# DLRM tower on one core: the Gram products spread, quad by quad, between the records of picks and of layer 1

## The reference

```
e = stack([tbl_f[ids[:, f]] for f in 0..31], axis=1)      # 2048 x 32 x 256, fp32
z[b, (i,j)] = dot(e[b, i], e[b, j]) for all i < j          # 496 dots a sample
h = concat([z, dense_ctx], axis=1)                         # 496 + 16 columns
h = relu(h @ W_top1 + b_top1)                              # 512 -> 512
h = relu(h @ W_top2 + b_top2)                              # 512 -> 256
y = h @ W_top3                                             # 256 -> 1
```

## Time and profile before

| what | value |
|---|---|
| median of three runs | 666.28 us (663.17 to 668.51) |
| the profiled execution's own time | 661.49 us |
| its span, first to last instruction | 659.5 us |
| mean granted TensorE clock | 0.966 |
| TensorE: matmuls busy, weight loads busy | 562.8 us (85%), 513.6 us (78%) |
| GpSimd, VectorE, ScalarE busy | 415.1 us, 297.7 us, 247.4 us |
| HBM read | 70.65 MB |

### The profile page before, as it was taken

One profiled execution on the slowest core, in us unless ns is written; L12 is line 12 of the kernel. 1 busy time (PEld: TensorE's weight loads), 2 busy tenths in 40 slices (PEclk: granted clock), 3 DMA queues, 4 the chain that ended last, 5 costly groups with the idle time before them and its releaser, 6 DMA issues.

```text
span 659.5 us, 26697 instructions
## 1 busy us (share of the span) xinstructions
PE 562.8 (85%) x12304; PEld 513.6 (78%) x12304; DVE 297.7 (45%) x556; ACT 247.4 (38%) x496; POOL 415.1 (63%) x435
## 2 busy tenths in 40 slices
PE   1453888999899999999898998999899899986885
PEld 0342888988888888999797988889798888885775
DVE  2144365556435355655435555654435555423041
ACT  1252244444243343433343343433334343334361
POOL 6787577766657576675757566675657667575400
PEclk9995799999999999999999999999999999998987
DMA  5559554433424243342534244242523333232200
GB/s 153 203 193 243 178 151 124 113 99 89 130 83 115 82 116 112 88 124 83 134 87 118 85 105 121 83 122 85 131 79 113 99 90 115 79 108 75 66 12 4
DMA packets 26244, 72.39 MB, mean 110 GB/s; under 512 B 8023, under 2 KB 8935, under 8 KB 25256
## 3 DMA queue, kind: packets, MB, share of 16 engines
q0 software_dynamic: 20544, 56.13, 30.7%
q1 hardware_dynamic: 5590, 14.57, 6.9%
HBM read 70.65 MB, written 0.01 MB: 107 GB/s over the span
## 4 chain that ended last, share of the span: by engine, by line
PE 76%; issue 10%; POOL 6%; ACT 5%; DMA 2%; DVE 1%; SPq 0%; ACTq 0%
PE ps_l L331 17%; PE ps_gram L298 16%; PE ps_pick L276 13%; PE ps_pick L278 12%; PE ps_turn L263 12%; POOL rows L249 6%; PE ps_l L344 4%; DMA rows<-in_table,index 2%; ACT cols L501 1%; ACT pairs L521 1%; DVE pairs L647 1%; ACT cols L467 1%; ACT stage L494 1%; ACT hidden L511 0%; PE ps_turn L361 0%
## 5 line engine op out<-in xcount | busy, mean ns | idle before, releaser
L249 POOL DMA_INDIRECT rows<-in_table,index x428 | 414.3, 968 | 210.5 <-issue 107.0
L647 DVE COPY pairs<-ps_gram 32x112 f32<-32x112 f32 (+1 forms) x480 | 180.6, 376 | 146.1 <-PE ps_gram L298 140.0
L471 ACT COPY cols<-ps_turn 128x512 f32<-128x512 f32 x194 | 114.6, 592 | 254.3 <-PE ps_turn L263 252.9
L263 PE MATMUL ps_turn<-identity,rows 128*128 128x128 f32 x856 | 142.4, 290 | 43.4 <-DMA rows<-in_table,index 41.3
L276 PE MATMUL ps_pick<-one_hot,table_hi 125*128 125x256 f32 x672 | 174.4, 297 | 1.0 <-ACT stage L494 0.8
L635 DVE TENSOR_TENSOR one_hot<-ps_wide,row_number 125x2048 fp32r<-125x2048 f32 x42 | 96.2, 2291 | 162.3 <-ACT ps_wide L488 139.0
L278 PE MATMUL ps_pick<-one_hot,table_lo 125*128 125x256 f32 x672 | 166.9, 286 | 0.0
L263 PEld LDWEIGHTS ps_turn<-identity,rows 128*128 128x128 f32 x856 | 102.5, 147 | 55.9 <-DMA rows<-in_table,index 34.8
L298 PE MATMUL ps_gram<-cols 128*32 128x32 f32 x7936 | 116.1, 202 | 32.4 <-issue 24.4
L298 PEld LDWEIGHTS ps_gram<-cols 128*32 128x32 f32 x7936 | 94.5, 111 | 58.9 <-issue 51.3
L276 PEld LDWEIGHTS ps_pick<-one_hot,table_hi 125*128 125x128 f32 x672 | 129.9, 193 | 2.2 <-issue 1.5
(11 more groups left out here) (51 smaller groups left out, 115.1 us busy)
## 6 DMA issues: line engine op xcount, KB each, us to landing
rows<-in_table,index POOLq DMA_INDIRECT x428
pick_id<-in_pick_ids SPq DMA_DIRECT2D x21, 250.0 KB
stage<-in_tbl SPq DMA_DIRECT2D x4, 1000.0 KB
w_sb<-in_w_t SPq DMA_DIRECT2D x1, 2048.0 KB, 28.5
w_sb<-in_tbl SPq DMA_DIRECT2D x2, 1000.0 KB
w_sb<-in_W_top SPq DMA_DIRECT2D x1, 512.0 KB
pairs<-in_dense_t SPq DMA_DIRECT2D x16, 8.0 KB, 1.6
scores<-score SPq DMA_DIRECT2D x16, 0.5 KB
```

Of the source, the lines that this page charges most:

```text
L249: pool.indirect_dma_start(out=rows[x % ROWS][:, k, :], out_offset=None, in_=table, in_offset=bass.IndirectOffsetOnAxis(ap=index[:, t, i:i ...
L263: last = pe.transpose(ps_turn[x % TURNS][:, h, SPG * k:SPG * (k + 1), :], rows[x % ROWS][:, k, h * P:(h + 1) * P], identity[:, :])
L471: act.copy(cols[t % COLS][:, :, :, FPU * u:FPU * (u + 1)], ps_turn[x % TURNS][:, :, :, :]).then_inc(cols_ready, 1)
L647: last = dve.tensor_copy(pairs[n % 2][N_FIELDS * q:N_FIELDS * (q + 1), c0:KC, TQ * j + FQ * u:TQ * j + FQ * (u + 1)] .rearrange("p c g -> ...
```

## The change

Nothing is added to or taken from what is computed. Four things move:

1. `pick` and `layer1` get three more arguments and call `gram` for a single quad after every second step c of their own loop, that is after every 4 of their 16 matmuls. Eight calls of a pair of blocks carry 4 quads each: in an even block the picks in units 0, 1, 3 and 4, in an odd block the second half of the pick (unit 1) and layer 1's parts in units 2, 3 and 4. `gram_parts` keeps bursts for block 1 (four quads in each of units 1 to 4), four quads in block 29 and the last two blocks.
2. TensorE's picks go to units 0, 1, 3 and 4 of even blocks and to units 0 and 1 of odd ones; layer 1's four parts go to units 2 to 5, layer 2 from unit 3 to unit 2, layer 3 from unit 6 to unit 5.
3. ScalarE's `take_pick`, `spread_ids`, `place`, `relu1`, `relu2` and `take_score` follow to the matching units. `relu1` is now in unit 5, ahead of `evacuate` of unit 6; `place` is in unit 5 for every block from 4 on.
4. VectorE makes both one-hot columns of an even block ahead of that block's `regroup`.

```diff
     def gram_parts(t):
         if t >= BLOCKS - 2:
             return {0: (0, FQ // 2), 1: (FQ // 2, FQ)}
-        return {2: (0, 8), 3: (8, 16)} if t % 2 == 1 else {0: (0, 6), 1: (6, 11), 3: (11, 16)}
+        if t < 2:
+            return {u: (4 * u - 4, 4 * u) for u in range(1, 5)}
+        if t == BLOCKS - 3:
+            return {1: (0, 4)}
+        return {}
...
-            def pick(q, h):
+            def pick(q, h, b=0, g0=0, quads=0):
...
-                if h == HALVES - 1:
-                    last.then_inc(picked, 1)
+                    if c == VC - 1 and h == HALVES - 1:
+                        last.then_inc(picked, 1)
+                    if c % 2 == 1 and c // 2 < quads:
+                        gram(b, g0 + c // 2, g0 + c // 2 + 1)
...
-            def layer1(n, m0=0, m1=M1C):
+            def layer1(n, m0=0, m1=M1C, b=0, g0=0, quads=0):
...
-                if m1 == M1C:
-                    last.then_inc(l1_done, 1)
+                        if c == KC - 1 and m == M1C - 1:
+                            last.then_inc(l1_done, 1)
+                        if c % 2 == 1 and c // 2 < quads:
+                            gram(b, g0 + c // 2, g0 + c // 2 + 1)
...
-                    if 3 <= t < BLOCKS - 1 and t % 2 == 1:
-                        if u == 0:
-                            layer1((t - 3) // 2, 0, 1)
-                        if u == 1:
-                            layer1((t - 3) // 2, 1, 2)
-                        if u == (4 if t == BLOCKS - 3 else 6):
-                            layer1((t - 3) // 2, 2, M1C)
+                    if t % 2 == 1 and jobs(t):
+                        if u in (0, 1):
+                            pick(jobs(t)[0], u, t - 1, 0, 4 * u)
+                        if u in (6, 7) and len(jobs(t)) == 2:
+                            pick(jobs(t)[1], u - 6)
+                    if 3 <= t < BLOCKS - 1 and t % 2 == 1 and 2 <= u < 2 + M1C:
+                        layer1((t - 3) // 2, u - 2, u - 1, t - 1, 4 * (u - 1), 4 if u < 5 else 0)
+                    if t % 2 == 0 and jobs(t):
+                        if u in (0, 1):
+                            pick(jobs(t)[0], u, t - 1, 4 * u, 4)
+                        if u in (3, 4):
+                            pick(jobs(t)[1], u - 3, t - 1, 4 * (u - 1), 4)
                     if 4 <= t and t % 2 == 0:
-                        if u == (0 if t == BLOCKS - 2 else 3):
+                        if u == (0 if t == BLOCKS - 2 else 2):
                             layer2((t - 4) // 2)
-                        if u == (2 if t == BLOCKS - 2 else 6):
+                        if u == (2 if t == BLOCKS - 2 else 5):
                             layer3((t - 4) // 2)
...
-                    if t > BPG and (t - 1) % BPG == 0 and u == 0:
-                        place(t - 1)
                     if t % 2 == 0 and t >= 2 and jobs(t):
                         a, b = jobs(t)
-                        if u == 1 and t > 2:
+                        if u == 0 and t > 2:
                             spread_ids(b)
-                        if u == 2:
+                        if u == 1:
                             take_pick(a)
-                        if u == 3 and b + 1 < JOBS:
+                        if u == 2 and b + 1 < JOBS:
                             spread_ids(b + 1)
-                        if u == 5:
+                        if u == 4:
                             take_pick(b)
...
-                    if t > BPG and t % BPG != 0 and u == (2 if t == BLOCKS - 1 else 5):
+                    if t >= BPG and u == (2 if t == BLOCKS - 1 else 5):
                         place(t)
-                    if 3 <= t < BLOCKS - 1 and t % 2 == 1 and u == (4 if t == BLOCKS - 3 else 6):
+                    if 3 <= t < BLOCKS - 1 and t % 2 == 1 and u == 5:
                         relu1((t - 3) // 2)
...
                 if t % 2 == 0 and t > 2 and jobs(t):
                     make_one_hot(jobs(t)[1])
+                    if jobs(t)[1] + 1 < JOBS:
+                        make_one_hot(jobs(t)[1] + 1)
...
                 regroup(t - 1)
-                if t % 2 == 0 and jobs(t) and jobs(t)[1] + 1 < JOBS:
-                    make_one_hot(jobs(t)[1] + 1)
```

More of the change, by code:

```diff
@@ L578, in _ @@
                         c = jobs(t)[-1]
-                        if t < SETTLED:
-                            if u == 0:
+                        if u == 1:
+                            take_pick(jobs(t)[0])
+                            if t < SETTLED:
                                 spread_ids(c)
-                            if u == 3:
-                                take_pick(c - 1)
-                        if u == (4 if t < SETTLED else 2):
+                        if u == 7:
+                            take_pick(c)
+                        if u == (5 if t < SETTLED else 2):
                             spread_ids(c + 1)
-                        if u == 5:
-                            take_pick(c)
-                    if t > BPG and t % BPG != 0 and u == (2 if t == BLOCKS - 1 else 5):
+                    if t >= BPG and u == (2 if t == BLOCKS - 1 else 5):
                         place(t)
-                    if 3 <= t < BLOCKS - 1 and t % 2 == 1 and u == (4 if t == BLOCKS - 3 else 6):
+                    if 3 <= t < BLOCKS - 1 and t % 2 == 1 and u == 5:
                         relu1((t - 3) // 2)
                     if 4 <= t and t % 2 == 0:
-                        if u == (0 if t == BLOCKS - 2 else 3):
+                        if u == (0 if t == BLOCKS - 2 else 2):
                             relu2((t - 4) // 2)
-                        if u == (2 if t == BLOCKS - 2 else 6):
+                        if u == (2 if t == BLOCKS - 2 else 5):
                             take_score((t - 4) // 2)
@@ L700, in _ @@
                     make_one_hot(jobs(t)[1])
+                    if jobs(t)[1] + 1 < JOBS:
+                        make_one_hot(jobs(t)[1] + 1)
+                if t == 2:
+                    make_one_hot(2)
                 if t % 2 == 1 and jobs(t):
```

## The result

The changed kernel's median is 710.99 us (709.91 to 712.77, 4 runs) against 665.09 us (663.17 to 668.51, 4 runs): the ratio is 1.069, with a 95% interval of 1.063 to 1.074. It is slower by 46 us. The profiled execution took 711.15 us, with a span of 709.1 us (from its first to its last instruction). The forecast was 721 us, in a range of 680 to 750.

A forecast was written before the change was run, and what follows sets the result against it. TensorE's time was taken to bound the kernel. Terms of 58 - 10 + 6 = +54 us took the profiled 661.49 us to 716, a forecast median of 721 us, 8% slower, in a range of 680 to 750.

The forecast's parts named there:

- The price of a quad on its own: On TensorE, a lone quad between long matmuls costs 0.45 us, 0.405 ahead of transposes; 196 us against 137.6 before, +58 us.
- Free entry: Rival: Gram weights load while the pick still runs, giving 40 us back, 681 us; chance 0.10.
- the faster rival: Rival: loads ahead of time hide a lone quad's entry and exit, 0.255 us a quad, 638 us; chance 0.08.
- The stalls: In Gram bursts TensorE runs out of issued instructions, 53 us; spreading quads between long matmuls was credited with winning it all.
- The rival in which they stay: Rival: instructions come late in the same places, the 53 us are not won, 774 us, with half 748; chance 0.09.
- The score: Layer 1's wait for the score, 10.2 us in 14 times, goes as layers 3 and 1 move apart: -10 us.
- ScalarE's order: relu1 ahead of the odd block's last evacuate makes the first quad wait 0.4 to 0.5 us in 13 even blocks: +6 us.
- The last blocks are as before: The last two blocks were taken as unchanged, with no term in the sum.
- the cover: In odd blocks TensorE has over 8 us of work before layer 1, against regroup's 6.2 us; enough by 2 us.
- the step to the median: The profiled run stands 4.8 us under the median of three runs, so 716 us profiled became a 721 us median.

The follow-up runs named there:

- e_moves: Changed kernel's order of records, but Gram products in bursts of 5 to 8 quads as in the kernel before: 632.05 us, ratio 0.948 to the kernel before.
- e_relu: Changed kernel with relu1 one unit later, behind the copy of the odd block's last unit: 706.93 us, ratio 1.062 to the kernel before.
- e_pairs: Changed kernel with two quads together after every 8 matmuls of a record instead of one after every 4: 633.38 us, ratio 0.954 to the kernel before.
- e_fours: Changed kernel with all four quads of a call together behind the record's 16 matmuls: 609.59 us, ratio 0.917 to the kernel before.
- e_moves_behind: e_moves with each burst behind the unit's record of long matmuls instead of ahead of it: 613.03 us, ratio 0.919 to the kernel before.
- e_between: Kernel before, with layer 1's first two parts in units 2 and 3 of odd blocks instead of 0 and 1: 660.86 us, ratio 0.995.
- e_fours_relu: e_fours with relu1 one unit later: 611.25 us, ratio 0.915 to the kernel before.
- e_moves_relu: e_moves with relu1 one unit later, behind the copy of the odd block's last unit: 624.30 us, ratio 0.937 to the kernel before.
- e_halves: Changed kernel with half a quad (8 matmuls) after every 2 matmuls of a record: 885.16 us, ratio 1.332 to the kernel before.

## Why the prediction was right, and where it was off

**The price of a quad on its own: right.** It was built from three changes of width in the trace of before, though none of them had a pick ahead of the quad, and the entry taken by the nearest row (0.21 us) is 194.25 to 194.46. A pick with four quads takes 3.70 us from its first start to the next transposes, a bare one 1.99, so 1.71; layer 1's part takes 3.51 for 1.79, so 1.72. The forecast had 3 x 0.45 + 0.405 = 1.755. Over 111 calls that is 190 us for 195. Free entry and the faster rival fall with the same rows.

**The stalls: right in the sum, wrong in what frees them.** 53 us were credited in full, and inside the single quads between 60 and 640 us no gap over 0.15 us is left. The rival in which they stay falls. What the forecast did not see is that the moves alone would free about half of these (39.2 to 20.0 us, above). The sum is not touched, since the term after is none either way. But the account that the 53 us are won by spreading is wrong: against e_moves, spreading wins the remaining 20 or so and the wait, and pays over 100. The time comes out the same; the reason does not.

**The score: right in the changed kernel, not tested alone.** Waits of 10.2 us became one of 2.2 us at the end, 8 us less where 10 were booked.

**ScalarE's order: right.** The Gram line waits for the copy in 12 even blocks, 0.36 us each, 4.3 us in all; the forecast had 0.4 to 0.5 us in 13, 6 us. (The other two of the 14 waits, 0.8 us each, stand in the last blocks.) e_relu gave 4 us back. (ScalarE's busy share in the earlier trace rows is 38%, not 39; nothing hangs on it.) ScalarE's and TensorE's timelines at one of them:

```profile
191.14 1.14 ACT L515 ACTIVATE hidden<-ps_l,b_sb 128x128 f32<-128x128 f32 x4 [0.46 <-PE ps_l L338]
192.16 0.39 ACT L471 COPY cols<-ps_turn 128x256 f32<-128x256 f32 x1
192.60 0.33 PE L305 MATMUL ps_gram<-cols 128*32 128x32 f32 x16 [0.36 <-ACT cols L471]
```

**Missed: block 29.** "The last blocks are as before" overlooked that block 29 has no picks. Layer 1 in its unit 2 has no pick between it and `regroup`, and so lacks most of the cover, "a pick, a pick with four quads", that I had named for the odd blocks:

```profile
630.34 0.71 PE L338 MATMUL ps_l<-pairs,w_sb 128*128 128x128 f32 x4 [2.39 <-DVE pairs L648]
630.98 0.34 PE L305 MATMUL ps_gram<-cols 128*32 128x32 f32 x16
631.25 1.23 PE L338 MATMUL ps_l<-pairs,w_sb 128*128 128x128 f32 x4
632.41 0.44 PE L305 MATMUL ps_gram<-cols 128*32 128x32 f32 x16
```

It waits 2.39 us, the granted clock falls to half right behind it, and the next three cycles take 1.53 us instead of 0.9.

**The size: 46 us for 54.** Between the two profiled executions it is 661.49 to 711.15, 50 us: 4 too many. The quad's price alone was 5 too high (195 for 190); the smaller misses (2 us of score left, 2 of copy not met, some 4 at block 29) go both ways and were not balanced one by one. The rest is the step to the median. The profiled execution of before was 4.8 us under its median, and I carried that over. The kernel before spreads over 11 us from run to run (660.9 to 672.1 in 23 runs), the changed one over 3 (709.9 to 712.8), so its profiled run is its median. That the spread comes from the stalls is not shown: e_pairs and e_fours, which have almost none, spread over 3 us too, but e_relu, without any, spreads over 5, and e_moves_behind, with 18 us of them, over less than 2.

**Why the moves alone halve the stalls.** The forecast had TensorE run out of issued instructions. For the long stalls the traces bear that out. Sort the gaps above by length. In the kernel before, 17 gaps of 0.6 to 2.0 us make 20.6 us and 78 of up to 0.3 us make 18.6; in e_moves 3 long ones make 3.2 us and 72 short ones 16.8. So nearly all that the moves free is long gaps. Count TensorE's records (loads, matmuls, semaphore waits) from the start of the trace: all 17 long gaps stand at the same place modulo 256 (192 or 193), and so do those of e_moves and of e_between. The page of the kernel before counts the transfers of instructions:

```profile
q8 instruction: 97, 1.59, 1.0%
```

That is 16.4 KB each, and TensorE has 24931 such records, 257 for each transfer. In the trace's records of that queue each of the 17 gaps ends 1.19 to 1.50 us after a transfer has ended, and the 15 of e_moves and e_between 1.23 to 1.56 us after one; by chance a gap would end there in about 6% of the cases. Both together say that a long gap is the wait for the next 256 instructions.

It comes where the last 256 went by fast. Of the 73 portions between 90 and 560 us, 23 took under 3 us in the kernel before, leaving out the gap at their end; the two bursts of eight quads, with only four transposes between them, hold such portions. 21 of the 23 end inside a burst, and 16 of these with a long gap; of the 31 slower ones that end inside a burst, one does. In e_moves 5 portions are that fast, and in e_pairs, e_fours and the changed kernel none, nor is there a long gap in those 470 us.

**Open.** In e_between 11 portions are that fast, and yet 12 long gaps make 16.9 us, three of them behind slower portions, so speed is not all that decides. By burst, the second burst of odd blocks fell from 1.4 us of stall to 0.5 with the moves, and to 1.0 in e_between, where it varies from pair to pair between 0.3 and 2.2. And what makes the short gaps, in the kernel before about half of them between the 60th and the 80th matmul of a burst, and nearly as many with the moves as without, no run here separates.

The fastest version measured is e_fours, at 609.6 us against 664.7 in the same set; e_fours_relu is not told apart from it.

## What to carry to other kernels

Count the changes of array width in a record, not only its matmuls: here each stretch of narrow products cost 0.33 us however short, as much as 40 of its own matmuls. Put short products together as far as they run through, here 64 (bursts of 80 and 96 had a gap each, and 64 was the longest tried below that), and put a record of long matmuls in front. And look at how fast instructions go by, not only at how long they take: before the change, 256 of them in under 3 us ended in a wait for the next ones in 16 places of 21. Last, measure the parts of a change by themselves: this one hid 33 us won by the moves behind 79 lost by the spreading, and four quads in place of one turned 7% slower into 8% faster.

## What the runs showed of the hardware

- A matmul of another width starts 0.07 to 0.08 us before the modelled end of the one under way, whatever that one is: a transpose, a Gram product, a one-column layer 3 and a pick. Layer 3's moving side is 128 columns like a transpose's, so it is the weights' width that counts.
- TensorE waits for its instructions in portions of 256. All 33 gaps of over 0.4 us within bursts that begin between 90 and 560 us, in the traces of before, e_moves, e_between and e_moves_relu, stand at one place modulo 256 records, and end 1.2 to 1.6 us after a transfer of 16.4 KB on the instruction queue.
- The granted clock fell to half in the middle of a busy stretch. In e_halves TensorE counts as busy throughout this window, and yet its clock (behind the five engines' columns) was 0.50, 1.2 GHz:

```profile
179.90:193.60 13.70, 13.70 (x126) 10.53 (x125) 1.94 (x2) 2.52 (x4) 2.76 (x4) 0.50 0.11 34
```

  It ran there in two such stretches, 27 us together, and in a third of 24 us behind a wait of 2.33 us for `regroup`, the one that block 29 has in the changed kernel too, with 7 us at half clock. No half clock is in the changed kernel between 68 and 631 us. Half of the 51 us in e_halves, less what the changed kernel pays, is about 22, and with the 147 us above it makes up most of the 174. That the clock counts the changes of width as idle is not shown: both falls came about 3 us after a wait of 0.6 us for columns, and the nine other waits of that kind and length before 770 us were followed by none.
- TensorE's busy share did not rank the kernels: 91% at 711 us, 85% at 665, and in e_fours and e_pairs it is 100% of ten pairs at 33.9 and 35.7 us a pair. The weight loads' busy share did: 72% in e_halves, 77% in the changed kernel, 78% before, 81% in e_pairs and e_moves, 83% in e_fours.
